# VectorE instead of GpSimd adds epsilon and negates the mean in every layer norm

## The chip, the cores and the metric

The kernel runs on one core of one Trainium2 chip, in one launch. The metric is the device time in microseconds of that core; lower is better. The engines are called as the profile calls them: PE is TensorE's matmul unit and PEld its weight load, DVE is VectorE, ACT is ScalarE, POOL is GpSimd, SP is SyncE, which issues the transfers.

## What is computed

The reference is a chain of four transformer-like layers on an input of 8 x 256 x 128 floats. Each half layer is `x = x + block(layernorm(x))`:

```
def _layernorm(x, axis=-1, eps=1e-05):
    m = jnp.mean(x, axis=axis, keepdims=True)
    v = jnp.var(x, axis=axis, keepdims=True)
    return (x - m) / jnp.sqrt(v + eps)
```

The blocks are, in order: attention on spike counts, a feed-forward block with weights and activations quantized to 4 bits, four Mamba layers (each with its own norm and a recurrence over 256 steps), a ternary feed-forward block, linear attention, a top-1 mixture of eight experts, a long convolution followed by a second norm, and a feed-forward block with retrieved experts. So each chunk of rows passes eight norms at the head of a half layer, four inside the Mamba layers and one inside the convolution block.

## The kernel before

The 2048 rows of x stay in SBUF, in a tile X. The batch is worked through in 8 chunks of 256 rows, each of them as two blocks of 128 rows on the partitions. A chunk goes through all half layers one after the other; different chunks are in different half layers at the same time. The work is cut into "lines", each with its own semaphores: `U` is the setup, `F` prepares the Mamba layers (its tiles print as `m`), `S` runs their recurrence (scan), and `a` and `b` are two workers for all other half layers (tiles `o`); `c` and `d` help at the end. What each engine does in which order is written out by hand: the table `ORDER` holds for every engine a string of letters, one letter per turn of a line. An engine works through its string strictly in order, so an instruction that waits holds up everything behind it on that engine, whichever line that belongs to.

The scan fills the middle of the run. For each of 32 units it has 8 groups of 128 x 1024 values: ScalarE makes the decay factors (L1036), VectorE makes the products `dtuB` (L1053, in PSUM) and scans over them (L1061, `tensor_tensor_scan`), GpSimd multiplies the result by C (L1071, in place in SBUF, both inputs from SBUF), and TensorE sums (L1090). The groups alternate with the two workers' instructions, norms among them.

A norm runs over three engines. `norm_dve` has VectorE take the statistics of each 128-row block (L361, `bn_stats`, and L364, `bn_aggr`, which leaves mean and variance side by side in `v.mv`). `norm_pool` has GpSimd add epsilon to the variances (L371), multiply the means by -1 (L372), raise variance plus epsilon to the power -1/2 (L374) and multiply minus the mean by that (L376). The constants -1/2, epsilon and -1 lie in a small tile `mhalf`. `norm_act` has ScalarE apply scale and bias to the rows (L381). L372 writes to `v.nb`, and L376 overwrites it in place. For most norms there are two blocks, so each of these small operations is 128 x 2; the last half layer of the last two chunks is split over two workers each, and those four norms have one block (128 x 1). In all 106 norms run.

Of the kernel before, what the change touches and what calls it, by code (L numbers as in the profile page):

```python
# [10 lines left out]
ALU = mybir.AluOpType  # L11
# [7 lines left out]
EPS = 1e-5  # L19
# [236 lines left out]
def program(nc, ap):  # L256
    with ExitStack() as ctx:
        def sb(name, shape, dt=F32):
            return ctx.enter_context(nc.sbuf_tensor(name, shape, dt))
# [35 lines left out]
        mhalf = sb("mhalf", [128, 6])  # L295
# [62 lines left out]
        def norm_dve(e, n, T, v, src, p=""):  # L358

            for i in range(v.blocks):  # L360
                e.bn_stats(v.st[:, i, :], src[:, i, :]).then_inc(T.dve, n.tick(f"{p}st{i}"))  # L361
            for i in range(v.blocks):
                e.wait_ge(T.dve, n.dve(f"{p}st{i}"))
                e.bn_aggr(v.mv[:, i, :], v.st[:, i, :]).then_inc(T.dve, n.tick(f"{p}mv{i}"))  # L364
            yield

        def norm_pool(e, n, T, v, p=""):

            b = v.blocks
            e.wait_ge(T.dve, n.dve(f"{p}mv{b - 1}"))  # L370
            e.tensor_tensor(v.ve, v.mv[:, :, 1], mhalf[:, 2:2 + b], ALU.add).then_inc(T.pool, n.tick(f"{p}ve"))  # L371
            e.tensor_tensor(v.nb, v.mv[:, :, 0], mhalf[:, 4:4 + b], ALU.mult).then_inc(T.pool, n.tick(f"{p}ng"))  # L372
            e.wait_ge(T.pool, n.pool(f"{p}ve"))
            e.tensor_tensor(v.rs, v.ve, mhalf[:, 0:b], ALU.pow).then_inc(T.pool, n.tick(f"{p}rs"))  # L374
            e.wait_ge(T.pool, n.pool(f"{p}rs"))
            e.tensor_tensor(v.nb, v.nb, v.rs, ALU.mult).then_inc(T.pool, n.tick(f"{p}nb"))  # L376
# [225 lines left out]
        class L0Attn(Stage):  # L602
# [17 lines left out]
            def dve(self, e, n, c):  # L620
                v, T = self, self.T
                if not n.dve():
                    e.wait_ge(loaded["const"], 16)
                    if T is Os[1]:
                        e.wait_ge(U.dve, U.at(0, "dve", "wq"))
                enter_dve(e, n, T, c, False)
                e.wait_ge(x_in[c // 2], 16)
                yield from norm_dve(e, n, T, v, X2(c))
                e.wait_ge(T.act, n.act("k"))
                yield from spikes_dve(e, n, T, v.cur, v.acc, v.qk, "c")  # L630
                e.wait_ge(loaded["l0a"], 16)
                e.wait_ge(T.pe, n.pe("v"))
                e.tensor_tensor(v.xn, ps2(T.banks[0]), row(w("l0a", "vb")), ALU.add).then_inc(T.dve, n.tick("v"))
                e.wait_ge(T.dve, n.dve("v"))
                yield from spikes_dve(e, n, T, v.xn, v.va, v.va, "u")
                e.wait_ge(T.dve, n.dve("c3"))
                for j in range(4):
                    e.tensor_scalar(v.km[j], v.qk[:, 1, :], hj[:, j:j + 1], None, ALU.mult).then_inc(T.dve, n.tick(f"m{j}"))
                yield
                yield from divide_dve(e, n, T, T.banks[0], v, 4.0, ALU.mult)  # L640
                e.wait_ge(T.pool, n.pool("ob"))
                e.wait_ge(T.pe, n.pe("o"))
                e.tensor_tensor(X2(c), ps2(T.banks[0]), X2(c), ALU.add).then_inc(T.dve, n.tick("x"))
                yield

            def pool(self, e, n, c):
                v, T = self, self.T
                if not n.dve():
                    e.wait_ge(U.pool, U.at(0, "pool", "mhalf"))
                norm_pool(e, n, T, v)  # L650
                yield
                e.wait_ge(T.act, n.act("xn1"))
                e.wait_ge(loaded["l0a"], 16)
                e.tensor_tensor(X2(c), X2(c), row(w("l0a", "ob")), ALU.add).then_inc(T.pool, n.tick("ob"))
                yield
                e.wait_ge(T.dve, n.dve("u3"))
                e.wait_ge(U.pool, U.at(0, "pool", T.name))
                spread_pool(e, n, T, v.va)
                yield
# [79 lines left out]
        class L0Ffn(Stage):  # L739
# [10 lines left out]
            def dve(self, e, n, c):  # L750
                v, T = self, self.T
                enter_dve(e, n, T, c, False)
                yield from norm_dve(e, n, T, v, X2(c))
                e.wait_ge(T.act, n.act("xn1"))
                yield from quant_dve(e, n, T, flat(v.xn), 16, v.q, "a")
                for i in range(2):
                    e.wait_ge(T.act, n.act(f"g{i}"))
                    e.wait_ge(T.pe, n.pe(f"u{i}"))
                    e.tensor_tensor(v.h[:, i, :], T.banks[0][:, 0:352], v.g[i], ALU.mult).then_inc(T.dve, n.tick(f"h{i}"))
                    yield  # L760
                e.wait_ge(T.dve, n.dve("h1"))
                yield from quant_dve(e, n, T, flat(v.h), 44, v.hq, "h")
                e.wait_ge(T.pe, n.pe("d"))
                e.tensor_tensor(X2(c), ps2(T.banks[0]), X2(c), ALU.add).then_inc(T.dve, n.tick("x"))
                yield

            def pool(self, e, n, c):
                norm_pool(e, n, self.T, self)
                yield
# [71 lines left out]
        class Front(Stage):  # L841


            def dve(self, e, n, k):
                v, b = chains[k % 2], F.bank
                if k >= 2:
                    c, l = UNITS[k - 2]
                    e.wait_ge(S.pe, S.at(k - 2, "pe", "y7"))
                    e.tensor_tensor(v.dtu, halves_of(S.y), v.z, ALU.mult).then_inc(F.dve, n.tick("y"))
                    yield  # L850
                    e.wait_ge(F.pe, n.pe("wo"))
                    e.tensor_tensor(v.hs, ps2(b), v.hs, ALU.add).then_inc(F.dve, n.tick("hs"))
                    e.wait_ge(F.dve, n.dve("hs"))
                    if l == NL - 1:
                        e.tensor_tensor(X2(c), X2(c), v.hs, ALU.add).then_inc(F.dve, n.tick("X"))
                        if k < NU:
                            e.wait_ge(F.dve, n.dve("X"))
                    yield
                if k >= NU:
                    return  # L860
                c, l = UNITS[k]
                if l == 0:
                    from_, job = before[c]
                    e.wait_ge(from_.dve, from_.done(job))
                    yield from norm_dve(e, n, F, v, X2(c), "h")
                    e.wait_ge(F.act, n.act("hxn1"))
                yield from norm_dve(e, n, F, v, v.hs)
                e.wait_ge(F.act, n.act("ln"))
                e.scalar_tensor_tensor(v.dt, v.dt, 0.0, halves_of(b), ALU.max, ALU.add).then_inc(F.dve, n.tick("dt"))  # L869
                yield  # L870
# [20 lines left out]
            def pool(self, e, n, k):  # L891
                v = chains[k % 2]
                if k == 0:
                    e.wait_ge(U.pool, U.at(0, "pool", "mhalf"))
                if k >= NU:
                    return
                c, l = UNITS[k]
                if l == 0:
                    norm_pool(e, n, F, v, "h")
                    yield  # L900
                norm_pool(e, n, F, v)
                yield
                e.wait_ge(F.dve, n.dve("dt"))
                e.tensor_tensor(v.dtu, v.dt, v.u, ALU.mult).then_inc(F.pool, n.tick("dtu"))  # L904
                yield
# [1109 lines left out]
        for c in (NB - 2, NB - 1):  # L2015
            T = next(T for T, s, d in todo if d == c and s is L3Attn)
# [143 lines left out]
```

## Time and profile before

| | us |
|---|---|
| median of 3 runs | 1813.95 |
| lowest, highest | 1809.46, 1826.51 |
| profiled execution, its own time | 1814.12 |
| its span, first to last instruction | 1812.3 |
| DVE busy | 1454.1 |
| POOL busy | 1194.4 |
| ACT busy | 1338.6 |
| PE busy | 1457.2 |

The span is what the trace covers; the execution's own time has 1.8 us more around it. A busy time is the union of an engine's instructions; a span on POOL is rough. The chain of waits is followed back from the last instruction of the run: at each step to what released it, or to the instruction before it on the same engine.

### The profile page before, as it was taken

To read this page: it belongs to the slowest core of one execution; us is meant where nothing else is said; L and a number is where in the kernel's file an instruction comes from. 1 tells how busy PE (TensorE), PEld (TensorE's weight loads), DVE (VectorE), ACT (ScalarE), POOL (GpSimd) and SP (SyncE) were. 2 spreads that over 40 slices of the span, in tenths; PEclk is the share of its full clock that TensorE was granted. 3 is DMA by queue.
4 is the path that set the end of the run, shared out by engine and by line. 5 is a ranking of instruction groups with operands and counts; after the bars stand their busy time and mean duration, and the time that the engine had idled before them with its cause. 6 is when DMAs were issued, how large, how long until landed. Compare 5 with 4: busy or idle time off the path is not lost.

```text
span 1812.3 us, 27075 instructions
## 1 busy us (share of the span) xinstructions
PE 1457.2 (80%) x9321; PEld 1033.3 (57%) x9321; DVE 1454.1 (80%) x2218; ACT 1338.6 (74%) x2745; POOL 1194.4 (66%) x991
## 2 busy tenths in 40 slices
PE   5676677667899986576888999778899987589985
PEld 2343334345677764344556777556667765467874
DVE  4789999999888898879998679787888998831138
ACT  4468666767898887777787878788898887664455
POOL 4148658876777688877667477778778887740125
PEclk6678768778999998676898999989999998699987
DMA  5023413424343542220444444231445532123310
GB/s 198 1 72 79 117 41 77 109 71 111 124 135 95 172 114 61 71 71 27 108 104 120 113 139 123 83 109 44 139 136 137 164 88 71 45 61 88 94 36 6
DMA packets 84616, 170.08 MB, mean 94 GB/s; under 512 B 9472, under 2 KB 14976, under 8 KB 84096
## 3 DMA queue, kind: packets, MB, share of 16 engines
q1 hardware_dynamic: 84480, 168.36, 33.9%
q8 instruction: 75, 1.23, 0.3%
q14 instruction: 61, 0.50, 0.1%
HBM read 99.11 MB, written 2.10 MB: 56 GB/s over the span
## 4 chain that ended last, share of the span: by engine, by line
PE 40%; DVE 26%; ACT 17%; POOL 7%; issue 6%; DMA 3%; SPq 0%; DVEq 0%; POOLq 0%; ACTq 0%
DVE m L1061 11%; DVE dtuB L1053 5%; ACT m L1036 5%; PE ps L1453 4%; PE ps L975 4%; ACT L352 4%; PE ps L1465 4%; PE ps L1324 3%; PE ps L1090 3%; POOL m L1071 2%; PE ps L1192 2%; PE ps L1335 2%; DMA m<-m 2%; PE ps L722 1%; ACT o L679 1%
## 5 line engine op out<-in xcount | busy, mean ns | idle before, releaser
L1071 POOL TENSOR_TENSOR m<-m 128x1024 f32<-128x1024 f32 x256 | 771.2, 3017 | 95.8 <-DVE m L1061 95.4
L1061 DVE TENSOR_TENSOR_SCAN m<-m,dtuB 128x1024 f32<-128x1024 f32 x256 | 584.7, 2284 | 22.6 <-ACT m L1036 9.9
L1036 ACT ACTIVATE m<-m,Aneg 128x255 f32<-128x255 f32 x1024 | 428.2, 497 | 27.3 <-DMA m<-m 26.2
L1053 DVE TENSOR_TENSOR dtuB<-m 128x1024 f32<-128x1024 f32 x256 | 344.7, 1346 | 13.2 <-DMA m<-m 6.6
L352 ACT ACT_TABLE_LOAD x189 | 242.5, 1283 | 3.4
L371 POOL TENSOR_TENSOR o<-o,mhalf 128x2 f32<-128x2 f32 (+1 forms) x64 | 19.9, 311 | 223.3 <-DVE o L364 223.1
L1090 PE MATMUL ps<-m,w_const 128*32 128x256 f32 x2048 | 146.2, 412 | 7.3 <-POOL m L1071 7.1
L1434 ACT ACTIVATE o<-ps,w_mo 128x256 f32<-128x256 f32 x256 | 106.5, 471 | 56.5 <-PE ps L1457 56.5
L1453 PE MATMUL ps<-o 128*128 128x256 f32 x512 | 138.5, 393 | 9.3 <-ACT o L1434 7.6
L975 PE MATMUL ps<-m,wc 128*128 128x256 f32 x512 | 136.8, 426 | 8.6 <-ACT m L392 8.5
L1465 PEld LDWEIGHTS ps<-o 128*128 128x128 f32 x1024 | 128.8, 191 | 16.2 <-issue 4.5
L1465 PE MATMUL ps<-o 128*128 128x128 f32 x1024 | 136.7, 277 | 0.4 <-DMA o<-in_mox 0.2
L1192 PE MATMUL ps<-o 128*128 128x256 f32 x512 | 122.7, 387 | 13.0 <-issue 5.1
L975 PEld LDWEIGHTS ps<-m,wc 128*128 128x128 f32 x512 | 108.3, 216 | 33.7 <-ACT m L392 12.9
L679 ACT ACTIVATE o<-ps 128x512 f32<-128x512 f32 x112 | 66.3, 593 | 71.5 <-PE ps L722 46.4
L722 PE MATMUL ps<-o 32*128 32x256 bf16 x224 | 57.7, 353 | 71.0 <-ACT o L679 57.9
L1192 PEld LDWEIGHTS ps<-o 128*128 128x128 f32 x512 | 93.8, 191 | 34.7 <-issue 15.5
L1090 PEld LDWEIGHTS ps<-m,w_const 128*32 128x32 f32 x2048 | 67.8, 117 | 71.6 <-issue 24.7
L1453 PEld LDWEIGHTS ps<-o 128*128 128x128 f32 x512 | 88.4, 190 | 30.1 <-ACT o L1434 15.9
L904 POOL TENSOR_TENSOR m<-m 128x512 f32<-128x512 f32 x32 | 48.7, 1522 | 58.9 <-DVE m L869 58.9
L1777 PE MATMUL ps<-w_const,o 128*128 128x128 f32 x192 | 39.2, 355 | 53.9 <-DVE o L1645 32.3
L722 PEld LDWEIGHTS ps<-o 32*128 32x128 bf16 x224 | 13.5, 99 | 116.6 <-ACT o L679 69.0
(363 smaller groups left out, 2892.2 us busy)
## 6 DMA issues: line engine op xcount, KB each, us to landing
m<-m SPq DMA_DIRECT2D x256, 256.0 KB, 5.0
m<-spread SPq DMA_DIRECT2D x64, 512.0 KB, 4.9
o<-in_mox SPq DMA_DIRECT2D x128, 256.0 KB, 3.8
o<-in_l1x SPq DMA_DIRECT2D x88, 256.0 KB, 3.0
w_mb<-in_mb SPq DMA_DIRECT2D x1, 2288.0 KB, 11.8
m<-in_cwr SPq DMA_DIRECT2D x1, 2048.0 KB, 15.9
w_l3f<-in_l3f SPq DMA_DIRECT2D x1, 1536.0 KB, 17.4
X<-in_x SPq DMA_DIRECT2D x4, 256.0 KB, 7.1
```

Of the source, the lines that this page charges most:

```text
L352: e.preload_act_table_set(SETS[kind])
L722: op = e.matmul(score[h % len(score)][:, kt * CH:kt * CH + CH], v.km[j][32 * g:32 * g + 32, cut(kt)], v.qk[32 * g:32 * g + 32, 0, :], star ...
L975: op = e.matmul(b[:, h * CH:h * CH + CH], wc[:, l, j, h * 128:h * 128 + 128], v.xT[:, j:j + CH], start=j == 0, stop=j == 3)
L1036: op = e.activation(dA[at % NA][:, j, 1:CH], R[q][:, h * CH + 1:h * CH + CH], ACT.Exp, scale=Aneg[:, l, 4 * g + j:4 * g + j + 1])
L1053: e.tensor_tensor(dtuB[:, :, :], bc(R[q][:, (2 + h) * CH:(3 + h) * CH].unsqueeze(1), 4, CH), Br[k % 2], ALU.mult).then_inc(S.dve, n.tick(f ...
L1061: e.tensor_tensor_scan(flat(G[at % NG]), flat(dA[at % NA]), flat(dtuB[:, :, :]), 0.0, ALU.mult, ALU.add).then_inc(S.dve, n.tick(f"s{g}"))
L1071: e.tensor_tensor(G[at % NG], G[at % NG], Cr[k % 2], ALU.mult).then_inc(S.pool, n.tick(f"c{g}"))
L1090: op = e.matmul(S.y[32 * q:32 * q + 32, h * CH:h * CH + CH], red, G[(8 * k + g) % NG][:, j, :], start=False, stop=j == 3, skip_group_check ...
L1192: op = e.matmul(b[:, 0:CH], v.ring[(at + j) % RING][:, cut(k)], src[:, k, :], start=k == 0, stop=k == 3)
L1434: e.activation(v.hd[p % 2][:, j, :], T.banks[1][:, j * CH:j * CH + CH], ACT.Relu, bias=w("mo", "b1")[:, p // 2, k:k + 1]).then_inc(T.act, ...
L1453: e.matmul(b[:, j * CH:j * CH + CH], v.ring[p // 2 * 2 % MRING][:, cut(p % 2 * 2 + j)], v.xT, start=j == 0, stop=False, skip_group_check=True)
L1465: op = e.matmul(a[:, cut(i)], v.hd[p % 2][:, j, cut(i)], v.ring[(p // 2 * 2 + 1) % MRING][:, cut(p % 2 * 2 + j)], start=False, stop=p == 1 ...
```

## The change

The two small operations that come directly behind the statistics move from GpSimd to VectorE. On VectorE they are `tensor_scalar` operations with a constant in the instruction, placed in the same turn as the statistics, with a wait on the last `bn_aggr` ahead of them. The source of each is every second word of `v.mv`. GpSimd waits for the second of them and goes on with the power; its wait for its own addition is gone. The constants for epsilon and -1 in `mhalf` are still written in the setup.

```
             for i in range(v.blocks):
                 e.wait_ge(T.dve, n.dve(f"{p}st{i}"))
                 e.bn_aggr(v.mv[:, i, :], v.st[:, i, :]).then_inc(T.dve, n.tick(f"{p}mv{i}"))
+            e.wait_ge(T.dve, n.dve(f"{p}mv{v.blocks - 1}"))
+            e.tensor_scalar(v.ve, v.mv[:, :, 1], EPS, None, ALU.add).then_inc(T.dve, n.tick(f"{p}ve"))
+            e.tensor_scalar(v.nb, v.mv[:, :, 0], -1.0, None, ALU.mult).then_inc(T.dve, n.tick(f"{p}ng"))
             yield
 
         def norm_pool(e, n, T, v, p=""):
 
             b = v.blocks
-            e.wait_ge(T.dve, n.dve(f"{p}mv{b - 1}"))
-            e.tensor_tensor(v.ve, v.mv[:, :, 1], mhalf[:, 2:2 + b], ALU.add).then_inc(T.pool, n.tick(f"{p}ve"))
-            e.tensor_tensor(v.nb, v.mv[:, :, 0], mhalf[:, 4:4 + b], ALU.mult).then_inc(T.pool, n.tick(f"{p}ng"))
-            e.wait_ge(T.pool, n.pool(f"{p}ve"))
+            e.wait_ge(T.dve, n.dve(f"{p}ng"))
             e.tensor_tensor(v.rs, v.ve, mhalf[:, 0:b], ALU.pow).then_inc(T.pool, n.tick(f"{p}rs"))
             e.wait_ge(T.pool, n.pool(f"{p}rs"))
             e.tensor_tensor(v.nb, v.nb, v.rs, ALU.mult).then_inc(T.pool, n.tick(f"{p}nb"))
```

In the changed kernel the two operations are lines 366 and 367; L374, L376 and all later lines keep their numbers. The turns of `ORDER` are the same, so the only moves are these. VectorE's order around one norm of worker `a` or `b` amid the scan, at about 1486 us of the run before; first before, then changed:

```order
L1053 TENSOR_TENSOR dtuB<-m 128x1024
L361 BN_STATS o<-X 128x6 x2
L364 BN_AGGR o<-o 128x2 x2
L1061 SCALAR_TENSOR_TENSOR m<-m,dtuB 128x1024
L1053 TENSOR_TENSOR dtuB<-m 128x1024
```

```order
L1053 TENSOR_TENSOR dtuB<-m 128x1024
L361 BN_STATS o<-X 128x6 x2
L364 BN_AGGR o<-o 128x2 x2
L366 TENSOR_SCALAR o<-o 128x2
L367 TENSOR_SCALAR o<-o 128x2
L1061 SCALAR_TENSOR_TENSOR m<-m,dtuB 128x1024
L1053 TENSOR_TENSOR dtuB<-m 128x1024
```

The scan L1061 now stands behind the two new operations. GpSimd's order at the same norm, before and changed:

```order
L1071 TENSOR_TENSOR m<-m 128x1024 x2
L371 TENSOR_TENSOR o<-o,mhalf 128x2
L372 TENSOR_TENSOR o<-o,mhalf 128x2
L374 TENSOR_TENSOR o<-o,mhalf 128x2
L376 TENSOR_TENSOR o<-o 128x2
L1071 TENSOR_TENSOR m<-m 128x1024 x2
```

```order
L376 TENSOR_TENSOR m<-m 128x2
L374 TENSOR_TENSOR o<-o,mhalf 128x2
L376 TENSOR_TENSOR o<-o 128x2
L1071 TENSOR_TENSOR m<-m 128x1024 x2
L374 TENSOR_TENSOR o<-o,mhalf 128x2
L376 TENSOR_TENSOR o<-o 128x2
L1071 TENSOR_TENSOR m<-m 128x1024 x2
```

Here the power and the product directly follow the scan's multiplications (the piece shows the norm before this one too).

## Rows read from the trace of the kernel before

**Rows 1.** The page, part 1: busy us, share of the span, instructions.
```profile
span 1812.3 us, 27075 instructions
...
PE 1457.2 (80%) x9321; PEld 1033.3 (57%) x9321; DVE 1454.1 (80%) x2218; ACT 1338.6 (74%) x2745; POOL 1194.4 (66%) x991
```

**Rows 2.** Busy time by stretches of the run, us.
```profile
100.00:600.00 500.00, 386.85 (x2494) 245.64 (x2493) 456.40 (x526) 373.53 (x797) 361.54 (x240) 0.84 0.38 98
600.00:1100.00 500.00, 411.08 (x2665) 293.58 (x2664) 430.08 (x607) 394.56 (x817) 354.89 (x276) 0.88 0.37 101
1100.00:1600.00 500.00, 413.77 (x2662) 313.03 (x2661) 430.01 (x662) 414.23 (x818) 398.73 (x308) 0.92 0.37 100
```
The columns are: stretch, its length, busy us of PE, PEld, DVE, ACT and POOL (each with its instructions), granted clock of PE, DMA share, GB/s.

**Rows 3.** The page, part 4: the chain that ended last, by engine.
```profile
PE 40%; DVE 26%; ACT 17%; POOL 7%; issue 6%; DMA 3%; SPq 0%; DVEq 0%; POOLq 0%; ACTq 0%
```

**Rows 4.** The same chain in order of time: start, us, what.
```profile
5.17 0.23 DVE o L364 x2
...
1486.00 0.10 DVE o L364 x2
...
1757.46 0.19 DVE o L364
1757.72 0.19 POOL o L371
```

**Rows 5.** Groups of POOL: count, busy us, mean ns, idle before.
```profile
L371 POOL TENSOR_TENSOR o<-o,mhalf 128x2 f32<-128x2 f32 (+1 forms) x64 | 19.9, 311 | 223.3 <-DVE o L364 223.1
...
L372 POOL TENSOR_TENSOR o<-o,mhalf 128x2 f32<-128x2 f32 (+1 forms) x64 | 13.5, 211 | 0.0
```

**Rows 6.** Timeline of a norm that POOL waited for: start us, us.
```profile
77.63 0.30 DVE L364 BATCH_NORM_AGGREGATE o<-o 128x2 f32<-128x6 f32 x2
78.01 0.20 POOL L371 TENSOR_TENSOR o<-o,mhalf 128x2 f32<-128x2 f32 x1 [27.78 <-DVE o L364]
...
78.16 0.20 POOL L372 TENSOR_TENSOR o<-o,mhalf 128x2 f32<-128x2 f32 x1
78.31 0.69 POOL L374 TENSOR_TENSOR o<-o,mhalf 128x2 f32<-128x2 f32 x1
```

**Rows 7.** Timeline of the setup on DVE: small TENSOR_SCALAR.
```profile
59.98 0.23 DVE L555 TENSOR_SCALAR Apow<-Apow,asg 128x2 f32<-128x2 f32 x1
60.11 0.22 DVE L557 TENSOR_SCALAR Wrev<-Wrev,asg 128x2 f32<-128x2 f32 x1
60.37 0.23 DVE L555 TENSOR_SCALAR Apow<-Apow,asg 128x4 f32<-128x4 f32 x1
```

**Rows 8.** Timeline, a norm amid the scan: DVE, and POOL beside it.
```profile
1485.92 0.29 DVE L364 BATCH_NORM_AGGREGATE o<-o 128x2 f32<-128x6 f32 x2
1486.14 2.29 DVE L1061 TENSOR_TENSOR_SCAN m<-m,dtuB 128x1024 f32<-128x1024 f32 x1
...
1484.48 3.34 POOL L1071 TENSOR_TENSOR m<-m 128x1024 f32<-128x1024 f32 x1
1487.78 0.19 POOL L371 TENSOR_TENSOR o<-o,mhalf 128x2 f32<-128x2 f32 x1
```

**Rows 9.** Timeline, small one-source operations on DVE and POOL beside them.
```profile
611.02 1.49 DVE L1406 CAST o<-o 128x2 f32<-128x2 uint32 x1
...
607.74 4.75 POOL L1071 TENSOR_TENSOR m<-m 128x1024 f32<-128x1024 f32 x2
...
907.88 1.98 DVE L404 TENSOR_SCALAR o<-o 128x16 f32<-128x16 f32 x1
...
905.17 4.66 POOL L1071 TENSOR_TENSOR m<-m 128x1024 f32<-128x1024 f32 x2
...
L1406 DVE CAST o<-o x8: 168/168/1486, 542.0 to 1700.0; 128x2 f32<-128x2 uint32 x8
```

**Rows 10.** The page, part 5: the scan's groups on POOL and DVE.
```profile
L1071 POOL TENSOR_TENSOR m<-m 128x1024 f32<-128x1024 f32 x256 | 771.2, 3017 | 95.8 <-DVE m L1061 95.4
L1061 DVE TENSOR_TENSOR_SCAN m<-m,dtuB 128x1024 f32<-128x1024 f32 x256 | 584.7, 2284 | 22.6 <-ACT m L1036 9.9
```

**Rows 11.** Waits of POOL for the norms' statistics: us, times, longest.
```profile
POOL o L371 <- DVE o L364: 223.1, 34, 32.6
...
POOL m L371 <- DVE m L364: 78.8, 24, 9.9
```

More of the change, by code:

```diff
@@ L364, in norm_dve @@
                 e.bn_aggr(v.mv[:, i, :], v.st[:, i, :]).then_inc(T.dve, n.tick(f"{p}mv{i}"))
+            e.wait_ge(T.dve, n.dve(f"{p}mv{v.blocks - 1}"))
+            e.tensor_scalar(v.ve, v.mv[:, :, 1], EPS, None, ALU.add).then_inc(T.dve, n.tick(f"{p}ve"))
+            e.tensor_scalar(v.nb, v.mv[:, :, 0], -1.0, None, ALU.mult).then_inc(T.dve, n.tick(f"{p}ng"))
             yield
@@ L369, in norm_pool @@
             b = v.blocks
[L370 to L373, printed above, removed]
+            e.wait_ge(T.dve, n.dve(f"{p}ng"))
             e.tensor_tensor(v.rs, v.ve, mhalf[:, 0:b], ALU.pow).then_inc(T.pool, n.tick(f"{p}rs"))
```

## The prediction

> **What bounds the kernel now.** I read the page's busy shares first. VectorE is busy for 1454.1 us of 1812.3, GpSimd for 1194.4, and TensorE is as full as VectorE [rows 1]. The table by stretches shows where: from 100 to 600 us VectorE works 456.40 of 500 us, from 600 to 1100 it works 430.08 [rows 2]. So the change takes work from an engine with idle time and gives it to one with little. The chain that ended last says what a microsecond of each is worth: 26% of it is VectorE's, 7% GpSimd's, the rest TensorE, ScalarE, issue and transfers [rows 3]. No engine is the whole bound; work added to VectorE counts where the chain runs through it.
>
> Next I looked at the norms in that chain. The statistics' last step (L364) stands in it for 35 of the 106 norms; the first and the last are shown [rows 4]. GpSimd's first norm operation (L371) stands in it 22 times. Sorting by what follows: 14 norms go through both, 21 go through VectorE's statistics and on to VectorE's next work, 8 through GpSimd's part alone.
>
> **What goes and what comes.** GpSimd loses L371 and L372, 106 times each, with means of 311 and 211 ns on the o buffers [rows 5]. What it really gives up is seen where it was idle: L371 starts 0.08 us after the statistics end (77.93 to 78.01), L372 0.15 later, and L374, the power, at 78.31, that is 0.30 us after L371 [rows 6]. The long cases in the mean are waits for something else and don't go: the next GpSimd instruction inherits them.
>
> VectorE gains two TENSOR_SCALAR of 128x2, 106 times each. The nearest row is L555/L557 in the setup: 0.23 and 0.22 us, the second starting 0.13 after the first, a dependent one 0.04 after the end of what it waits for [rows 7]. L366 needs the statistics, so it starts 0.03 to 0.04 behind them; L367 needs nothing new. Without the change the next VectorE instruction starts 0.08 before the statistics' end, as L1061 does in [rows 8]. With it: 0.03 (wait) + 0.13 + 0.18 (L367, between 0.17 and 0.22) = 0.34 to L367's end, and the next one again starts 0.08 before that end, plus a little drain: I take **0.34 us** of VectorE per norm (0.30 to 0.40), 36.0 us for 106.
>
> The latency of a norm hardly moves. Before, the power starts 0.08 + 0.30 = 0.38 us behind the statistics. After, 0.34 for the two VectorE operations and 0.08 for the hand-over make 0.42. So the 0.30 us taken off GpSimd don't shorten the path to the power; they come back as GpSimd waiting. Only where a norm stands in GpSimd's queue long after its statistics are done does 0.30 us really go.
>
> **The term that decides.** The two new operations read and write SBUF with one source. In the trace such operations do not run while GpSimd works: the cast of 128x2 (L1406) normally takes 168 ns, but at 611.02 it took 1.49 us and ended at 612.51, when GpSimd's two L1071 (607.74 + 4.75 = 612.49) had ended [rows 9]. L404, a TENSOR_SCALAR of 128x16, took 1.98 us from 907.88, ending 0.03 behind the L1071 pair that ended at 909.83 [rows 9]. The statistics and the scan L1061 are not held up: L1061 has a mean of 2284 ns over 256, though GpSimd runs L1071 beside it nearly every time [rows 10]. So today the norm's VectorE part slips through beside GpSimd, and after the change it no longer can.
>
> How often? GpSimd was idle and waiting for the statistics at 34 + 24 = 58 norms [rows 11]; at the other 48 it had something else to do. Reading the timeline norm by norm, a GpSimd instruction that isn't a norm's was running at the statistics' end in 38 cases, and what it had left adds up to 31.5 us, 0.83 us each. The norm at 1486 us is such a case: statistics end at 1486.21, L1071 at 1487.82, so L366 would wait 1.6 us, and behind it stands L1061, the next link of the chain [rows 8]. The order of instructions shows nothing between them.
>
> Whether a TENSOR_SCALAR whose source has a step of two words waits as well is not in the trace: the operations seen to wait read words side by side. The bounds are no wait (0) and the full rest (31.5 us); I take the full rest, since the cast of the same 128x2 is the nearest row. The Trainium skill, "VectorE: DVE Perf Modes", section "Mode 2×_2P — use both read ports for one tensor", asks only for one source, SBUF on both sides and an even outermost dimension, not for a step of one. By that rule both operations take the port pair and wait; with a rule that excluded steps, the sum below would be that of the first rival.
>
> **The sum.** 21 norms where the chain stays on VectorE: 21 x 0.34 = 7.1 us, and 11 of them meet a running GpSimd instruction, with 9.7 us left: 16.8. The 14 that go on to GpSimd cost 0.04 each: 0.6. The 8 in GpSimd's part alone: 5 were queued behind other GpSimd work with the statistics just done. There the power now starts 0.03 + 0.13 + 0.18 + 0.08 = 0.42 behind that work instead of 0.30; the other 3 may gain 0.30. Together 0. The other 71 norms add 71 x 0.34 + 21.4 = 45.5 us to VectorE, of which the idle time that follows directly on some of them takes 13, read norm by norm. What is left, about 32 us, lies beside other work; that cover is thin in the dense stretch, and I let a tenth through: 3. **16.8 + 0.6 + 0 + 3 = 20 us.** The profiled execution took 1814.12 us, the median is 1813.95, so the sum stands on both alike: **1834 us**. Transfers, TensorE, ScalarE and SyncE keep their instructions and order.
>
> A measurement of this kernel can tell about 1% (18 us) from no change, so the forecast sits just beyond that line: 1832.1.
>
> **Rivals.**
> *The port is not taken* (chance 0.15). With the stepped source L366 and L367 slip through as the statistics do. The 9.7 us go: 7.1 + 0.6 + 2 = 10, **1824 us**. For it: no row has this form. Against: the cast.
> *The slack takes it* (0.16). 74% of the chain is not VectorE's [rows 3], and a chain delayed on VectorE can be overtaken by a parallel path that waits for TensorE or ScalarE a moment later. Then a fifth of 20 remains: **1818 us**. For it: 358 us of VectorE idle time. Against: only 44 to 70 us of it lie in each 500 us of the middle.
> *VectorE is the bound of the middle* (0.11). Then every microsecond counts: 36.0 + 31.5 less 14 that idle time takes = 53, **1867 us**. For it: 91% busy from 100 to 600. Against: the 26%.
> *GpSimd is what gates* (0.08), the one that ends faster. At the 48 norms where it was not idle, its queue gets 0.30 us shorter each: 48 x 0.30 = 14, **1800 us**. It decides only if VectorE finished its two operations before GpSimd's turn came, without a port wait. For it: those 48 norms. Against: mostly GpSimd was still in the very instruction that L366 must now wait for, and 7% of the chain. The Trainium skill, "GPSIMD Engine Reference", section "4.1 Engine selection", gives elementwise work to VectorE, GpSimd being about twice as slow with two inputs. At this size the rows don't agree: 0.20 us on GpSimd [rows 6], 0.22 on VectorE [rows 7].
>
> **Numbers.** The forecast's case (1824 to 1850) has 0.50. About a quarter of it ends under 1832.1, so slower by over 1% gets 0.37 + 0.11 = 0.48; within 1% is 0.13 + 0.15 + 0.16 = 0.44; faster 0.08. The range leaves out most of the faster case and of the full bound: 1810 to 1856.
>
> **What would show it.** VectorE's busy time near 1454 + 60 = 1515 us; L366's median near 180 ns but its mean near 0.4 to 0.5 us, with the long ones ending 0.03 behind a GpSimd L1071, L904, L1674 or L1679; L367 near 180 ns nearly always. GpSimd's busy time down by 40 to 56 us, but its idle time before L374 up by about as much. L1061, L1053 and L1071 unchanged in their means. The forecast fails if L366 never exceeds 0.25 us (the first rival), or if it does wait but VectorE's idle time shrinks by the same amount (the second).

## The result

| | before | changed |
|---|---|---|
| median, us | 1813.7 (4 runs) | 1834.57 (4 runs) |
| lowest, highest | 1809.46, 1826.51 | 1833.1, 1837.26 |
| profiled execution, span | 1812.3 | 1832.7 |

The changed kernel takes 1.0116 times as long, 95% interval 1.0092 to 1.0139. A second set of five runs, in e8 below, gave 1.0122 (1.0097 to 1.0147). So it is slower by 21 to 22 us, give or take 4, near the forecast of 1834.

The page of the changed kernel, its busy time and its chain by engine, is to be read beside [rows 1] and [rows 3]:

```profile
span 1832.7 us, 27075 instructions
...
PE 1468.7 (80%) x9321; PEld 1042.7 (57%) x9321; DVE 1497.2 (82%) x2430; ACT 1339.6 (73%) x2745; POOL 1162.7 (63%) x779
...
PE 41%; DVE 30%; ACT 15%; issue 7%; POOL 5%; DMA 2%; SPq 0%; DVEq 0%; POOLq 0%; ACTq 0%
```

VectorE is busy for 43.1 us more, GpSimd for 31.7 us less. VectorE's share of the chain went from 26% to 30%, GpSimd's from 7% to 5%. The statistics' last step now stands in the chain for 53 of the 106 norms, where it was 35. TensorE does the same 9321 multiplications and is busy for 11.5 us more; its mean granted clock was 0.879 to 0.880 over the runs of the kernel before and 0.874 and 0.876 over the two sets of the changed one. No run separates what that took from the rest.

The two new operations, all 106 of each, with the shortest, median and longest duration in ns:

```profile
L366 DVE TENSOR_SCALAR o<-o x64: 153/170/1818, 5.0 to 1780.6; 128x2 f32<-128x2 f32 x62, 128x1 f32<-128x1 f32 x2
L366 DVE TENSOR_SCALAR m<-m x42: 153/170/2182, 81.1 to 1781.2; 128x2 f32<-128x2 f32 x40, 128x1 f32<-128x1 f32 x2
...
L367 DVE TENSOR_SCALAR o<-o x64: 144/160/656, 5.0 to 1780.6; 128x2 f32<-128x2 f32 x62, 128x1 f32<-128x1 f32 x2
L367 DVE TENSOR_SCALAR m<-m x42: 144/160/164, 81.2 to 1781.3; 128x2 f32<-128x2 f32 x40, 128x1 f32<-128x1 f32 x2
```

The medians are alike, the longest are not. Of the 106 L366, 31 took over 0.26 us; what they took beyond 0.18 us adds up to 23.9 us. Each of the 31 ended 0.02 to 0.03 us behind a GpSimd instruction that ran as it began: 21 times L1071, 7 times L1679, once each L520, L904 and L1674. L367, right behind it, waited once. Here is one, in the timeline (start us, us) of VectorE and then of GpSimd, at the place of [rows 8]:

```profile
1507.47 0.30 DVE L364 BATCH_NORM_AGGREGATE o<-o 128x2 f32<-128x6 f32 x2
1507.81 1.59 DVE L366 TENSOR_SCALAR o<-o 128x2 f32<-128x2 f32 x1
1509.32 0.16 DVE L367 TENSOR_SCALAR o<-o 128x2 f32<-128x2 f32 x1
1509.38 2.27 DVE L1061 TENSOR_TENSOR_SCAN m<-m,dtuB 128x1024 f32<-128x1024 f32 x1
...
1505.98 3.40 POOL L1071 TENSOR_TENSOR m<-m 128x1024 f32<-128x1024 f32 x1
1509.55 0.69 POOL L374 TENSOR_TENSOR o<-o,mhalf 128x2 f32<-128x2 f32 x1 [0.18 <-DVE o L367]
```

L1071 ends at 1509.38, L366 at 1509.40. In [rows 8] the scan began 0.22 us after the start of the group L364; here it begins 1.91 us after. GpSimd then stands for 0.18 us until L367 is done. Over the whole run it waited for L367 at 93 norms, where it had waited for the statistics at 58 [rows 11]:

```profile
POOL o L374 <- DVE o L367: 240.2, 56, 32.9
...
POOL m L374 <- DVE m L367: 89.6, 37, 10.3
```

Those are 329.8 us against 301.9 before. GpSimd has 31.7 us less to do and stands 27.9 us longer before its norm work. Of the scan's own groups, against [rows 10], L1061 is unchanged and L1071 takes 7.5 us more in all, 1%:

```profile
L1071 POOL TENSOR_TENSOR m<-m 128x1024 f32<-128x1024 f32 x256 | 778.7, 3046 | 114.8 <-DVE m L1061 114.6
L1061 DVE TENSOR_TENSOR_SCAN m<-m,dtuB 128x1024 f32<-128x1024 f32 x256 | 584.5, 2283 | 19.3 <-ACT m L1036 8.5
```

**The ledger.** I measured how far a norm pushes VectorE's next instruction back, at norms with no idle time behind them: from the start of the second L364 to the start of what follows. Before, it is 0.10 us. Changed, with the waits taken out, it is 0.37 us on the mean. So the fixed part is 0.266 us a norm, 28.2 us for 106; the waits beyond the operations' normal length are 24.4 us for both lines together. VectorE's order is pushed by 52.6 us in all, and the run is 21 to 22 us longer: **0.40 to 0.42 us of time per us of push.** The push counts all 106 norms, also the 23 in the changed kernel behind which VectorE had nothing ready at once.

### The profile page after: what moved, and what is told of

It is laid out like the page before. It is cut to its first block, busy times and chain, and to the rows that moved or that the text cites. A ratio compares the mean times of both kernels' runs of the same rounds, so it can differ in the third digit from the quotient of the medians.

```text
span 1832.7 us, 27075 instructions
## 1 busy us (share of the span) xinstructions
PE 1468.7 (80%) x9321; PEld 1042.7 (57%) x9321; DVE 1497.2 (82%) x2430; ACT 1339.6 (73%) x2745; POOL 1162.7 (63%) x779
## 4 chain that ended last, share of the span: by engine, by line
PE 41%; DVE 30%; ACT 15%; issue 7%; POOL 5%; DMA 2%; SPq 0%; DVEq 0%; POOLq 0%; ACTq 0%
DVE m L1061 12%; DVE dtuB L1053 6%; PE ps L1453 4%; ACT m L1036 4%; PE ps L1465 4%; ACT L352 3%; PE ps L1324 3%; PE ps L975 3%; PE ps L1090 3%; PE ps L1192 3%; POOL m L1071 2%; PE ps L1335 2%; PE ps L981 1%; PE ps L709 1%; PE ps L722 1%
## 5 line engine op out<-in xcount | busy, mean ns | idle before, releaser
L1071 POOL TENSOR_TENSOR m<-m 128x1024 f32<-128x1024 f32 x256 | 778.7, 3046 | 114.8 <-DVE m L1061 114.6
L1061 DVE TENSOR_TENSOR_SCAN m<-m,dtuB 128x1024 f32<-128x1024 f32 x256 | 584.5, 2283 | 19.3 <-ACT m L1036 8.5
L374 POOL TENSOR_TENSOR o<-o,mhalf 128x2 f32<-128x2 f32 (+1 forms) x64 | 50.6, 790 | 240.2 <-DVE o L367 240.2
L975 PE MATMUL ps<-m,wc 128*128 128x256 f32 x512 | 141.2, 437 | 8.2 <-ACT m L392 8.0
L374 POOL TENSOR_TENSOR m<-m,mhalf 128x2 f32<-128x2 f32 (+1 forms) x42 | 33.5, 797 | 89.6 <-DVE m L367 89.6
L904 POOL TENSOR_TENSOR m<-m 128x512 f32<-128x512 f32 x32 | 48.6, 1518 | 59.9 <-DVE m L869 59.9
```

The lines of the kernel that those rows point to most:

```text
L975: op = e.matmul(b[:, h * CH:h * CH + CH], wc[:, l, j, h * 128:h * 128 + 128], v.xT[:, j:j + CH], start=j == 0, stop=j == 3)
L1061: e.tensor_tensor_scan(flat(G[at % NG]), flat(dA[at % NA]), flat(dtuB[:, :, :]), 0.0, ALU.mult, ALU.add).then_inc(S.dve, n.tick(f"s{g}"))
L1071: e.tensor_tensor(G[at % NG], G[at % NG], Cr[k % 2], ALU.mult).then_inc(S.pool, n.tick(f"c{g}"))
```

## The experiments

Each kernel ran 4 to 6 times, e4 and e9 12 times, beside 11 or 17 runs of the kernel before on the same chip. The ratio is that to the kernel before, with its 95% interval; a time over before is what the ratio has above 1, times that kernel's 1813 to 1814 us. Lines of kernels with added lines are shifted by a few: L1072, L1075 or L1076 is the L1071 of the text.

**e1: the scalars from a tile.** Does the form with a scalar per partition avoid the wait?

```
-            e.tensor_scalar(v.ve, v.mv[:, :, 1], EPS, None, ALU.add).then_inc(T.dve, n.tick(f"{p}ve"))
-            e.tensor_scalar(v.nb, v.mv[:, :, 0], -1.0, None, ALU.mult).then_inc(T.dve, n.tick(f"{p}ng"))
+            e.tensor_scalar(v.ve, v.mv[:, :, 1], mhalf[:, 2:3], None, ALU.add).then_inc(T.dve, n.tick(f"{p}ve"))
+            e.tensor_scalar(v.nb, v.mv[:, :, 0], mhalf[:, 4:5], None, ALU.mult).then_inc(T.dve, n.tick(f"{p}ng"))
```

VectorE also waits once, at its start, for `mhalf` to be written.

> The changed kernel, but the two VectorE operations take epsilon and -1 from the small tile mhalf, as a scalar per partition, instead of a constant in the instruction. The trace shows operations of that form (L638, 128x256 bf16) beside a running GpSimd instruction 24 times and none longer than 284 ns. Theory (the extra 20.7 us are VectorE's work, and more than half of them the 23.9 us that L366 stood waiting for GpSimd's running instruction): L366 never exceeds 0.25 us, VectorE's busy time falls by some 24 us against the changed kernel, and the time to 1818 to 1826. Rival 1 (the waits lie beside other work; the fixed 0.2 us per norm and the later power are what costs): L366 short as well, but the time stays at 1830 to 1836. Rival 2 (it isn't the form that decides, every VectorE operation of one SBUF source waits): L366 still has some 30 cases over 0.26 us and the time stays at 1834.

Measured: 1843.81 us, 1.0148 (1.0125 to 1.0170). The theory's hope for this form fell, and rival 2 was right about the waits: again 31 long cases of L366, 21.7 us beyond the median. The ratio is 0.3% over that of the changed kernel, which the intervals don't clearly tell apart.

```profile
L366 DVE TENSOR_SCALAR o<-o,mhalf x64: 213/229/2033, 5.0 to 1791.0; 128x2 f32<-128x2 f32 x62, 128x1 f32<-128x1 f32 x2
...
L367 DVE TENSOR_SCALAR o<-o,mhalf x64: 202/222/1324, 5.2 to 1791.1; 128x2 f32<-128x2 f32 x62, 128x1 f32<-128x1 f32 x2
```

This form takes 0.06 us longer per operation. L367 starts 0.14 us behind L366, not 0.08, and six of them, not one, took over 0.26 us. Each of the six ended 0.02 to 0.03 us behind a GpSimd instruction, and five of these instructions had begun 0.01 to 0.03 us after the L367 that waited for them. One of the five (VectorE, then GpSimd):

```profile
436.42 0.54 DVE L366 TENSOR_SCALAR o<-o,mhalf 128x2 f32<-128x2 f32 x1
436.87 1.32 DVE L367 TENSOR_SCALAR o<-o,mhalf 128x2 f32<-128x2 f32 x1
...
434.58 2.35 POOL L1072 TENSOR_TENSOR m<-m 128x1024 f32<-128x1024 f32 x1 [0.20 <-DVE m L1062]
436.89 1.28 POOL L905 TENSOR_TENSOR m<-m 128x512 f32<-128x512 f32 x1
```

L366 waits out L1072, then L367 waits out L905. The push is 40.7 us fixed and 26.4 of waiting (both operations, beyond their medians), 67.1 in all, for 26.8 us of time: 0.40 per us, as in the changed kernel.

**e2 and e3: VectorE's cost without GpSimd's relief.** The kernel before with two operations whose results nobody uses, in the one form and in the other.

```
                 e.bn_aggr(v.mv[:, i, :], v.st[:, i, :]).then_inc(T.dve, n.tick(f"{p}mv{i}"))
+            e.wait_ge(T.dve, n.dve(f"{p}mv{v.blocks - 1}"))
+            e.tensor_scalar(v.s1, v.mv[:, :, 1], EPS, None, ALU.add).then_inc(T.dve, n.tick(f"{p}d1"))
+            e.tensor_scalar(v.s2, v.mv[:, :, 0], -1.0, None, ALU.mult).then_inc(T.dve, n.tick(f"{p}d2"))
```

> The kernel before, GpSimd's four operations kept, and behind the statistics two VectorE operations of the changed kernel's very form (constant in the instruction) whose results nobody uses. It has the changed kernel's VectorE cost without any relief of GpSimd, and without the norm waiting for them. Theory (the cost is VectorE's, the relief of GpSimd is worth nothing): 1830 to 1838, as the changed kernel. Rival (GpSimd's relief won back a part): 1840 or more, and the difference to the changed kernel is what the relief was worth. Rival (the cost is the norm's own path, later by what the operations take): near 1814 to 1820, since the norm doesn't wait for these two.

Measured: 1835.54 us, 1.0121 (1.0102 to 1.0140). That is the changed kernel's time. GpSimd still does all four operations, and the norms don't wait for VectorE's two. The two differences together come to nothing that these runs can tell; e4 below takes the first by itself.

> As the last one, with epsilon and -1 as scalars per partition from mhalf: VectorE's fixed cost alone, without the wait for GpSimd and without relief. Theory: 1818 to 1826, half way between before and changed, and within 3 us of the changed kernel with that form. Rival (only the port wait costs): 1814 to 1817. Rival (only the fixed part costs): 1832 or more.

Measured: 1847.07 us, 1.0188 (1.0165 to 1.0210). The expectation missed, for the same reason as e1: this form does wait. Push 42.5 + 26.0 = 68.5 us, time 34.1, or 0.50 per us. It is 0.4% over e1, where e2 and the changed kernel are equal. The trace has one thing more in e3: 63 of the 106 first operations end 0.02 us behind L375, which is GpSimd's own addition of epsilon (L371 of the text), after some 0.26 us instead of 0.23. That adds about 2 us of push, too little for the 7 us of time, so most of the difference stays open.

**e4: GpSimd's relief without VectorE's cost.** L371 and L372 are left out and nothing is put in their place; the kernel computes neither the epsilon nor the negation.

```
-            e.tensor_tensor(v.ve, v.mv[:, :, 1], mhalf[:, 2:2 + b], ALU.add).then_inc(T.pool, n.tick(f"{p}ve"))
-            e.tensor_tensor(v.nb, v.mv[:, :, 0], mhalf[:, 4:4 + b], ALU.mult).then_inc(T.pool, n.tick(f"{p}ng"))
-            e.wait_ge(T.pool, n.pool(f"{p}ve"))
-            e.tensor_tensor(v.rs, v.ve, mhalf[:, 0:b], ALU.pow).then_inc(T.pool, n.tick(f"{p}rs"))
+            e.tensor_tensor(v.rs, v.mv[:, :, 1], mhalf[:, 0:b], ALU.pow).then_inc(T.pool, n.tick(f"{p}rs"))
             e.wait_ge(T.pool, n.pool(f"{p}rs"))
-            e.tensor_tensor(v.nb, v.nb, v.rs, ALU.mult).then_inc(T.pool, n.tick(f"{p}nb"))
+            e.tensor_tensor(v.nb, v.mv[:, :, 0], v.rs, ALU.mult).then_inc(T.pool, n.tick(f"{p}nb"))
```

> The kernel before without GpSimd's addition of epsilon and without its negation of the mean, and nothing put in their place: the computation leaves out both, the power and the product read the statistics themselves. It prices the relief of GpSimd with no cost on VectorE: some 32 us less GpSimd work and every norm 0.3 us sooner. Theory (GpSimd does not gate; its chain share is 7%, 22 norms of 106 with 0.30 us each are 6.6 us): 1804 to 1811. Rival (GpSimd gates, and the change lost only by what it did to VectorE): 1800 or less. Rival (relief is worth nothing): 1812 to 1816.

Measured: 1813.03 us, 0.9998 (0.9977 to 1.0018). The last rival was right: the relief is worth nothing that shows, 4 us at the very most. The page of this run, against [rows 1], has GpSimd 34.5 us less busy and VectorE where it was:

```profile
PE 1456.0 (80%) x9321; PEld 1033.7 (57%) x9321; DVE 1452.7 (80%) x2218; ACT 1337.6 (74%) x2745; POOL 1159.9 (64%) x779
```

**e5: the fixed work without the wait.** Two more `bn_aggr`, an operation that was never seen to wait for GpSimd (`ident` is a constant tile, `sc` one whose contents nobody uses).

```
+            e.wait_ge(T.dve, n.dve(f"{p}mv{v.blocks - 1}"))
+            e.bn_aggr(sc[:, 0:2], ident[:, 0:6]).then_inc(T.dve, n.tick(f"{p}d1"))
+            e.bn_aggr(sc[:, 2:4], ident[:, 0:6]).then_inc(T.dve, n.tick(f"{p}d2"))
```

> The kernel before, with two more bn_aggr behind each norm's own (their input a constant tile, their results unused). In the trace bn_aggr never waits for GpSimd: 208 of them, none over 184 ns, many beside a running L1071. So this adds the fixed VectorE work of the change (0.26 us a norm by the changed kernel's trace, 28 us in all) without the 24 us of waiting. Theory (each microsecond that VectorE's order is pushed back costs 0.40 us, whether it is work or a wait: 20.9 of 28 + 24 = 52): 1814 + 0.40 x 28 = 1825, that is 1821 to 1829. Rival 1 (the port wait is the whole cost): 1812 to 1817. Rival 2 (the fixed work is the whole cost, the waits lie beside other work): 1831 to 1837.

Measured: 1827.43 us, 1.0074 (1.0054 to 1.0094). As the theory had it. The 106 first ones (here those of the o workers: shortest, median, longest) never waited:

```profile
L368 DVE BATCH_NORM_AGGREGATE scr_o<-w_const x66: 181/182/183, 4.8 to 1772.8; 128x2 f32<-128x6 f32 x66
```

And this is one that began while GpSimd was in the middle of two multiplications (VectorE, then GpSimd); compare it with L366 at 1507.81 above:

```profile
1498.22 0.30 DVE L365 BATCH_NORM_AGGREGATE o<-o 128x2 f32<-128x6 f32 x2
1498.55 0.18 DVE L368 BATCH_NORM_AGGREGATE scr_o<-w_const 128x2 f32<-128x6 f32 x1
1498.65 0.15 DVE L369 BATCH_NORM_AGGREGATE scr_o<-w_const 128x2 f32<-128x6 f32 x1
1498.71 2.25 DVE L1066 TENSOR_TENSOR_SCAN m<-m,dtuB 128x1024 f32<-128x1024 f32 x1
...
1494.33 5.80 POOL L1076 TENSOR_TENSOR m<-m 128x1024 f32<-128x1024 f32 x2
```

The push is 29.6 us, all of it fixed, and the time 13.4 us. e2 has the same fixed push (29.6) and 24.5 us of waiting on top, and takes 21.9 us. The waiting is thus worth 8.5 us, give or take 5 by the two intervals, and the fixed work 13.4, give or take 4. Both rivals are out: e5 is clear of no change, and its interval ends at 1830.4 us, under the 1831 of rival 2.

**e6 and e7: one operation, four operations**, unused, with the constant in the instruction, in e6 the first line only:

```
+            e.tensor_scalar(v.s1, v.mv[:, :, 1], EPS, None, ALU.add).then_inc(T.dve, n.tick(f"{p}d1"))
```

and in e7

```
+            for k, (at, value, op) in enumerate(((1, EPS, ALU.add), (0, -1.0, ALU.mult)) * 2):
+                e.tensor_scalar(sc[:, 2 * k:2 * k + v.blocks], v.mv[:, :, at], value, None, op).then_inc(
+                    T.dve, n.tick(f"{p}d{k}"))
```

> The kernel before, with only one unused TENSOR_SCALAR behind the statistics (constant in the instruction). It keeps the whole wait for GpSimd (in e2 the second operation waited for nothing) and has two thirds of the fixed work, the second operation started 0.08 us behind the first: 0.19 us a norm, 20 us, and 24 of waiting. Theory (0.40 per us): 1814 + 0.40 x 44 = 1832 (1828 to 1835). Rival 1 (only the wait costs): 1833 to 1836, as with two operations. Rival 2 (only the fixed work costs): 1826 to 1830.

Measured: 1832.92 us, 1.0106 (1.0090 to 1.0122). Push 21.8 + 22.9 = 44.7 us, time 19.2: 0.43 per us. The theory's 1832 holds, but the interval, 1829.7 to 1835.5 us, reaches into the ranges of both rivals. It is e5 that excludes them.

> The kernel before, with four unused TENSOR_SCALAR behind the statistics, two pairs of the changed kernel's form. Only the first should wait for GpSimd, so 24 us of waiting as before and 0.26 + 0.16 = 0.42 us of fixed work a norm, 45 us. Theory (0.40 per us): 1814 + 0.40 x 69 = 1842 (1838 to 1846). Rival 1 (only the wait costs): 1834 to 1837. Rival 2 (VectorE becomes the bound as it fills, each further us costs a whole one): 1835.5 + 17 = 1852 or more.

Measured: 1850.98 us, 1.0212 (1.0196 to 1.0229). The theory is out, 5 us beyond its range; rival 2 starts at 1852, inside this run's interval (1848.9 to 1854.9). Nor did only the first operation wait: the third took over 0.26 us at six norms. Push 45.5 + 28.1 = 73.6 us, time 38.5: 0.52 per us. From e2 to e7 the push grows by 19.5 us and the time by 16.6, that is 0.85 per us, between 0.6 and 1.1 by the intervals. That would fit a price that rises as VectorE fills, but e1 with 67.1 us of push still pays 0.40, so this is not shown. The two kernels that pay 0.50 and more, e3 and e7, also ran at the lowest mean granted clocks of TensorE, 0.872 and 0.870, where the others had 0.874 to 0.879. Whether the clock is a cause or follows from the longer waits was not tried.

**e8: the changed kernel again.**

> The changed kernel once more, to have it beside the others in five rounds. Theory: 1.0106 to 1.0125 of the kernel before, 1833 to 1837, within 3 us of e2 (the same VectorE work, GpSimd not relieved). Rival (relief is worth several us): 5 us or more under e2.

Measured: 1836.08 us, 1.0122 (1.0097 to 1.0147), beside e2's 1.0121.

**e9: the lesson turned round.** Another small VectorE operation goes to ScalarE.

```
-                    e.wait_ge(T.act, n.act(f"w{i}2"))
-                    e.tensor_tensor(v.Em[0][:, 511:512], v.Em[0][:, 511:512], v.w5, ALU.add).then_inc(T.dve, n.tick(f"a5{i}"))
...
+                            if h == 2:
+                                e.wait_ge(T.act, n.act(f"w{i}2"))
+                                e.activation(Eh[:, 511:512], Eh[:, 511:512], ACT.Identity, bias=v.w5).then_inc(
+                                    T.act, n.tick(f"a5{i}"))
```

> The lesson turned round, on the kernel before: another small VectorE operation of SBUF operands that waits for GpSimd is taken off VectorE. In the last block's feed-forward, L1645 adds one number per partition (128x1, 12 times, 133 ns at its shortest, 700 on the mean, up to 1841 beside L1071, and TensorE stood 32.3 us waiting for it); ScalarE does it as an Identity with a bias per partition, right behind the activation that it needs. Theory: VectorE loses 8.4 us of work and waits, worth 0.35 to 0.5 each, 3 to 4 us, and TensorE gets its operand up to 0.5 us sooner at 12 places: 1808 to 1812. Rival (ScalarE's added 3 to 4 us, or nothing on the path): 1813 to 1816.

Measured: 1812.36 us, 0.9984 (0.9962 to 1.0005). Not clear of no change. The page, against [rows 1]:

```profile
PE 1460.5 (81%) x9321; PEld 1036.5 (57%) x9321; DVE 1445.0 (80%) x2206; ACT 1344.5 (74%) x2757; POOL 1195.8 (66%) x991
```

VectorE gave up 9.1 us, ScalarE took on 5.9. The median lies between the theory's range and the rival's. The ratio is 2.9 us of gain, with an interval from 6.9 us of gain to 0.9 of loss, so this run decides between neither.

| | push of VectorE, us (fixed + waiting) | time over before, us | per us |
|---|---|---|---|
| e5 two bn_aggr | 29.6 + 0 | 13.4 | 0.45 |
| e6 one operation | 21.8 + 22.9 | 19.2 | 0.43 |
| changed | 28.2 + 24.4 | 21.0 | 0.40 |
| e2 two operations | 29.6 + 24.5 | 21.9 | 0.40 |
| e1 scalars from a tile | 40.7 + 26.4 | 26.8 | 0.40 |
| e3 the same, unused | 42.5 + 26.0 | 34.1 | 0.50 |
| e7 four operations | 45.5 + 28.1 | 38.5 | 0.52 |

## Why the prediction was right

**That the new operations wait for GpSimd** was right, and this was the step that no row of the form showed. 31 norms met it, where I had read 38 running instructions, and the waits are 23.9 us, not 31.5. The places were read rightly: in the changed kernel, too, an instruction that isn't a norm's was running at the statistics' end at 36 norms, with 30.4 us left in all. The error is that the rest was counted from the statistics' end, on top of the fixed work. L366 starts 0.04 us behind that end and takes 0.17 itself, so about the first 0.19 us of each rest costs nothing more. The same rests of the kernel before, less that, make 25.8 us, and 33 long cases. The rule that I cited from the Trainium skill, "VectorE: DVE Perf Modes", section "Mode 2×_2P — use both read ports for one tensor", asks for no step of one; the trace agrees for a step of two words, with 31 of 106 that took up to 2.18 us. Rival 1 is out.

**The fixed cost** was sized 0.34 us a norm and measured 0.266. L367 follows L366 after 0.08 us, not 0.13. My row for that was L555/L557, which takes its scalar from a tile; e1 shows that the form itself makes the difference (0.14 us from start to start, and 0.22 us per operation against 0.16).

**The split of the sum** was off, and its total is right in part by luck: two errors cancelled. I gave the fixed work 7.1 us through 21 norms of the chain, and 3 us for all work and waiting off it. e5 puts the fixed work at 13.4. The waits I had at 9.7 us, counted too long as said above, and e2 less e5 gives 8.5. The step that failed is the tenth that I let through of what lies off the chain. With 5.6 us for the 21 norms of the chain at 0.266, e5 leaves 7.8 us for the other 85, whose fixed work is 22.6: a third, between a fifth and a half by e5's interval. The chain of the changed kernel ran through the statistics of 53 norms, that of e5 through 49 and that of e7 through 63; it was 35 before, and 29 and 32 in e4 and e9, which add nothing to VectorE. So norms come onto the chain as VectorE is pushed, and a count on the old chain is too low. With the true 0.266 us in the same sum, and the 8.5 us of waiting, the forecast would have been 5.6 + 8.5 + 0.6 + 3 = 17.7 us, too low by a sixth.

**That GpSimd's relief is worth nothing** was right in the sum. e4 shows it (relief alone: 0.9998, at most 4 us). e2 beside e8 agrees (1.0121 without relief, 1.0122 with it), but there the norm also waits for VectorE's two operations, and the two effects could cancel. The fastest rival, 1800 us, is out. The section "4.1 Engine selection" of the Trainium skill's "GPSIMD Engine Reference" would send this work to VectorE. The rows speak of 0.20 us on GpSimd and 0.16 to 0.17 on VectorE, when VectorE does not wait; the mean of L366 with its waits is 0.40 (42.2 us over 106).

**That the latency of a norm hardly moves** holds as well. Where GpSimd stood waiting, the power starts 0.38 us behind the statistics before and 0.35 changed; the forecast had 0.38 and 0.42. Where L366 waits, GpSimd was still in the instruction that it waits for. And the power may come 0.3 us sooner at every norm (e4) with no effect that shows.

**The other rivals.** That slack takes four fifths of it (1818 us) is out by the result. VectorE as the bound with a full us per us is not the changed kernel's case (0.40); for the last 19.5 us of e7 it is not excluded. Of the signs that I named, VectorE's busy time rose by 43 us, not 60, since both terms were sized too large. GpSimd's fell by 31.7, not by 40 to 56: 106 times the 0.30 us that I had read between L371 and L374 make 31.8, and I should have used that here too. L1071 was to stay as it was and grew by 1%.

## What to carry to other kernels

Before moving a small operation from GpSimd to VectorE, ask what GpSimd will be doing when it comes up. A TENSOR_SCALAR with both sides in SBUF stood there until GpSimd's running instruction ended, at 31 of 106 norms, and everything behind it in VectorE's order stood too; a `bn_aggr` in the same place, also SBUF on both sides, never did. Count the push on the engine's whole order, not only on the old chain, and price it by a trial with work that changes nothing else, as the two `bn_aggr` did. Here a us of push cost 0.40 to 0.45 us in the kernels with up to 54 us of it, and 0.40 to 0.52 in the three with 67 to 74. Relief of GpSimd, which mostly stood waiting for VectorE before its norm work, was worth nothing that showed.

## What the runs showed of the hardware

The TENSOR_SCALAR of 128x2 with its scalar in a tile had a median of 229 and 222 ns against 170 and 160 with the constant in the instruction, and waited for GpSimd just the same (31 of 106 in both). The second of a pair waited once in the changed kernel, where it follows 0.08 us behind the first, and six times in e1, where it follows after 0.14; five of those six times for an instruction of GpSimd that had only just begun.

I had expected that the form of e1 would not wait, since L638, a 128x256 bf16 operation of that form, never took over 284 ns beside GpSimd in the kernel before. That row could not show it. There, 21 of the 32 L638 started beside a short copy of GpSimd (L434) that was over before L638 was, and three beside the power L374, which did not hold them. And L638 does wait: in the changed kernel and in e1, e3, e4 and e7 one of the 32 took 674 to 681 ns, each ending 0.08 us behind GpSimd's L654 (a 128x256 addition in SBUF; both lines are shifted by a few in some of these kernels). In the changed kernel:

```profile
L638 DVE TENSOR_SCALAR o<-o,w_const x32: 278/280/678, 15.8 to 861.0; 128x256 bf16<-128x256 bf16 x32
...
331.86 0.64 POOL L654 TENSOR_TENSOR X<-X,w_l0a 128x256 f32<-128x256 f32 x1
```
